# Attention's output products in three 16-bit terms, and a clamp written with two inputs

## The chip, the cores and the metric

The program runs on 1 core of one Trainium2 chip, in one launch. The metric is the device time of that core in microseconds, from the program's start to its end; lower is better. Three runs of the kernel before are shown, and one profiled execution, whose trace is read here.

## The reference, cut to what matters

Four layers follow one another on 2048 tokens of 128 numbers: an attention with 16 heads, a mixture of experts, a state space scan, and a second mixture. The change touches the attention alone, and in it the normalisation of queries and keys and the last product, `out @ w_out`.

```python
B, S, D, H, DH = 2, 1024, 128, 16, 64          # x as drawn: (2, 1024, 128)
q = (x @ w_q).reshape(b, s, h, -1).transpose(0, 2, 1, 3)
k, v = jnp.split(x @ w_kv, 2, axis=-1)
q = _l2norm(q) * jnp.exp(scale)                # t / max(norm(t), 1e-12), per head
k = _l2norm(k)
attn = jax.nn.softmax(jnp.einsum('bhid,bhjd->bhij', q, k), axis=-1)
out = jnp.einsum('bhij,bhjd->bhid', attn, v)
out = out.transpose(0, 2, 1, 3).reshape(b, s, h * out.shape[-1])
attention = out @ w_out + b_out

x = _layernorm(x + attention(x))
x = _layernorm(x + mixture_of_8_experts(x))    # top 2, silu gate, 512 wide
x = _layernorm(x + state_space_scan(x))
x = _layernorm(x + second_mixture(x))          # top 2 of 8, and a shared expert
```

## The kernel before, in words

**Tiling.** `attention` works on 16 halves `h`, each with two heads of one of the two sequences and 16 slots long. Two halves make a pair `i`, so there are 8 pairs, 0 to 7, of 32 slots. In a slot, the scores of 256 queries against 512 keys are made, exponentiated, and multiplied with the values. Slots 0 to 15 of a pair are its even half, slots 16 to 31 its odd half; while they run, the projections and normalisation of the next half are prepared. `heads` runs the function `slot(i, s)` of each engine over all of them, and then 32 more slots (`TAIL`) without scores for what is left over, the tail.

**What each engine does in slot s.** TensorE: 8 score matmuls (L510, L511) of slot s, 24 value matmuls (L536, L538, L540) of slot s-3 (`LAG`), and at set slots projections (L477 to L479), transposes of queries and keys (L492), transposes of finished outputs (L550) and the output products (L558). ScalarE: the exponential (L699), copies out of the accumulators (L668, L669, L681) and the copy `OT` of the turned outputs (L688). VectorE: the low part of the exponentials (L815), for every slot but 1 and 15 of a half; and at set slots the normalisation (L788, L797, L802), the sums of squares (L774), their clamp (L778), the division of finished outputs (L834, L838) and the addition of an output product to the residual stream (L847). GpSimd: the low parts for slots 1 and 15 (L1044), the power that gives inverse norms (L1051), low parts of values (L1059) and of normalised queries and keys (L1066). SyncE issues DMAs only.

**16-bit terms.** A product of 32-bit numbers is made in most places from three 16-bit products: high times high, high times low, low times high. The high part of a 32-bit tile that stays in place is its upper half read as bf16 (`high(...)[:, 1::2]`), the low part is the difference in f16. The output products (L558) are an exception: one matmul of 128x128 f32 for each of two blocks of 128 tokens, which the trace shows as two records each.

**Order.** Every engine runs its instructions in the order in which the code writes them, and waits on counting semaphores. The slots are tables of numbers: the output products of pair i, units u = 0 to 7, stand at `OUT_AT` = 41, 44, 47, 50, 57, 59, 61, 63, counted from the pair's first slot, so they run in the next pair at its slots 9, 12, 15, 18, 25, 27, 29 and 31; I name a product by its number here (P41 to P63). The turned outputs are read at `OUT_TURN_AT`. `SUM_AT` = 1, 4, 6, 8 places sum and clamp in each half, `NORM_AT` = 4, 6, 8, 10 the normalisation. Within a slot VectorE does the low part first, then the addition of a product, then normalisation and sum, then, every second slot, the division. TensorE may run ahead of VectorE: a value matmul of slot s-3 needs only that slot's low part.

**Waits around the change.** A product waits for its turned outputs (`s_out_turned_read`, ScalarE) and, since all products share the bank M0, for the addition of the one before (`s_out_added`, VectorE). In the tail two banks alternate. The clamp waits for its sum; the power on GpSimd waits for the clamp.

Of the kernel before, what the change touches and what calls it, by code (L numbers as in the profile page):

```python
# [4 lines left out]
F32 = mybir.dt.float32  # L5
# [25 lines left out]
def wait(eng, sem, count):  # L31

    if not isinstance(count, int) or count > 0:
        eng.wait_ge(sem, count)
# [29 lines left out]
TAIL = 32  # L64
RESIDUAL_AT = 14


# [47 lines left out]
def out_slot(u):  # L115

    return OUT_AT[u]


# [131 lines left out]
def attention(nc, io, t):  # L251
# [3 lines left out]
    def sb(name, shape, dt):  # L255
        return es.enter_context(nc.sbuf_tensor(name, shape, dt))
# [4 lines left out]
    with es:  # L261
# [3 lines left out]
        xT_lo = sb("xT_lo", [P, T], F16)  # L265
        wo = sb("wo", [P, H // 2 * D], F32)
        esc = sb("esc", [P, H], F32)
# [13 lines left out]
        Ob = sb("Ob", [P, NT, 2 * DH], F32)  # L281
        OT = sb("OT", [P, PJ, 2, P], F32)
        half = t["half"]
        bout = sb("bout", [P, D], F32)
# [37 lines left out]
        s_qk_high = sem("s_qk_high")  # L322
        s_k_copied = sem("s_k_copied")
        s_qk_low = sem("s_qk_low")
        s_turned = sem("s_turned")
# [102 lines left out]
        def _(eng):  # L428
            for c in range(WCH):
                eng.dma_start(w_f32[:, chunk(c)], io["wqkv"][:, chunk(c)]).then_inc(s_w_loaded[c], 16)  # L430
                if c == 0:
# [3 lines left out]
                    eng.dma_start(scl[:, :], io["scale"].partition_broadcast(P)).then_inc(s_loaded["scl"], 16)  # L435
            eng.dma_start(wo[:, :], io["wout"]).then_inc(s_loaded["wo"], 16)
            eng.dma_start(t["x"][:, :, :], io["x"].rearrange("(t p) d -> p t d", p=P)).then_inc(s_loaded["x"], 16)
# [19 lines left out]
        def _(eng):  # L457
# [95 lines left out]
            def out_product(i, u):  # L553

                wait(eng, s_out_turned_read, 8 * i + u + 1)
                for r in range(2):
                    pair = (2 * i + u // 4) % TB
                    mm = eng.matmul(out_bank(i, u)[:, P * r:P * r + P], OT[:, u, r, :],  # L558
                                    wo[:, D * pair:D * pair + D], start=True, stop=True)
                mm.then_inc(s_out_product, 1)  # L560
# [88 lines left out]
            for j in range(PJ):  # L649
                m1_free(0, j, 0, 0)  # L650
                transposes(0, j)
            eng.wait_ge(s_loaded["wo"], 16)
            eng.wait_ge(s_squares, PJ)
# [3 lines left out]
        def _(eng):  # L657
# [27 lines left out]
            def read_out_transposes(i, u):  # L685

                wait(eng, s_out_turned, 8 * i + u + 1)
                eng.activation(OT[:, u, :, :], out_turn_bank(i, u).rearrange("p (r c) -> p r c", r=2), ACT.Copy).then_inc(  # L688
                    s_out_turned_read, 1)
# [80 lines left out]
        def _(eng):  # L770
            def square_sums(h, hb, g):
                G, b = 4 * h + g, g % 2
                wait(eng, s_squares, 8 * h + 2 * g + 2)
                eng.tensor_reduce(ss[:, b, :, :], sq[:, b, :, :, :], AX, ALU.add).then_inc(s_square_sums, 1)  # L774

                wait(eng, s_square_sums, G + 1)
                wait(eng, s_inverse_norms, G - 1)
                eng.tensor_scalar(ss2[:, b, :, :], ss[:, b, :, :], 1e-24, None, ALU.max).then_inc(s_clamped, 1)  # L778

# [48 lines left out]
            def read_out(i, s):  # L828
# [10 lines left out]
                                  rden[:, u % 4, :].unsqueeze(2).to_broadcast([P, 2, DH]), ALU.mult).then_inc(  # L839
                                      s_outputs, 1)  # L840

            def add_out(i, u):
# [131 lines left out]
            def slot(i, s):  # L974
# [3 lines left out]
                if isinstance(i, int) and i == 0:  # L978

                    if s == RESIDUAL_AT:  # L980
                        start_residual()
                if (x := out_unit(s, out_slot)) and exists(i, x[0]):
                    if isinstance(i, int) and i < 2:
                        eng.wait_ge(s_residual, 1)
                    add_out(i - x[0], x[1])
# [1119 lines left out]
```

## Time and profile before

| | |
|---|---|
| median of 3 runs | 1048.07 us (1045.07 to 1051.78) |
| profiled execution | 1048.55 us, span 1046.8 us |
| TensorE busy | 914.1 us, 87% |
| ScalarE busy | 768.9 us, 73% |
| VectorE busy | 731.9 us, 70% |
| GpSimd busy | 499.3 us, 48% |
| attention | from 0 to about 636 us |

The span is the time from the first to the last instruction of the program; what is around it took 1.75 us in the profiled execution. Busy TensorE time is the union of matmuls whose ends are modelled, so that short waits between matmuls do not show in it; the starts of the matmuls in the timeline do. A short operation on VectorE starts some 0.08 us before the record of the one in front ends, so its step (start to start) is shorter than its record.

### The profile page before, as it was taken

To read this page: it belongs to the slowest core of one execution; us is meant where nothing else is said; L and a number is where in the kernel's file an instruction comes from. 1 tells how busy PE (TensorE), PEld (TensorE's weight loads), DVE (VectorE), ACT (ScalarE), POOL (GpSimd) and SP (SyncE) were. 2 spreads that over 40 slices of the span, in tenths; PEclk is the share of its full clock that TensorE was granted. 3 is DMA by queue.
4 is the path that set the end of the run, shared out by engine and by line. 5 is a ranking of instruction groups with operands and counts; after the bars stand their busy time and mean duration, and the time that the engine had idled before them with its cause. 6 is when DMAs were issued, how large, how long until landed. Compare 5 with 4: busy or idle time off the path is not lost. (4 is left out here: it accounts for less than half of the span.)

```text
span 1046.8 us, 34708 instructions
## 1 busy us (share of the span) xinstructions
PE 914.1 (87%) x13676; PEld 859.4 (82%) x13676; DVE 731.9 (70%) x1432; ACT 768.9 (73%) x1275; POOL 499.3 (48%) x384
## 2 busy tenths in 40 slices
PE   3789999999999999999999988979979479899930
PEld 2678998998999989888889988979968479899830
DVE  6699989888988988888998975325569849400202
ACT  5679998998988999988889865435563456687831
POOL 5475655555554654644778800413346350052423
PEclk9799999999999999999999998989989589899975
DMA  8400000000000000000001020713110030023111
GB/s 255 130 2 3 23 3 22 3 3 22 3 3 22 3 3 23 3 3 23 9 11 35 12 63 9 233 50 91 48 31 26 6 94 2 16 72 97 57 56 43
DMA packets 43563, 42.13 MB, mean 40 GB/s; under 512 B 5648, under 2 KB 37392, under 8 KB 43408
## 3 DMA queue, kind: packets, MB, share of 16 engines
q1 hardware_dynamic: 39312, 31.51, 10.1%
q0 software_dynamic: 4096, 8.40, 2.6%
q8 instruction: 116, 1.90, 0.7%
q14 instruction: 39, 0.32, 0.1%
HBM read 25.60 MB, written 14.29 MB: 38 GB/s over the span
## 5 line engine op out<-in xcount | busy, mean ns | idle before, releaser
L699 ACT ACTIVATE Pr<-SC,nesc,esc 128x1024 f32<-128x1024 f32 x256 | 310.2, 1212 | 33.3 <-PE SC L511 23.0
L815 DVE TENSOR_TENSOR Pl<-Pr 128x1024 f16<-128x1024 f32 x224 | 293.2, 1325 | 41.4 <-ACT Pr L699 39.7
L510 PE MATMUL SC<-QK 128*128 128x256 f16 x1024 | 239.2, 274 | 1.0 <-ACT QK L681 1.0
L511 PE MATMUL SC<-QK 128*128 128x256 f16 x1024 | 239.2, 274 | 0.0
L536 PE MATMUL OP<-V,Pr 128*128 128x65 f16 x2048 | 215.0, 193 | 6.1 <-DVE Ob L838 5.9
L538 PE MATMUL OP<-V,Pr 128*128 128x64 f16 x2048 | 215.8, 195 | 0.0
L540 PE MATMUL OP<-V,Pl 128*128 128x65 f16 x2048 | 214.6, 192 | 0.0
L536 PEld LDWEIGHTS OP<-V,Pr 128*128 128x128 bf16 x2048 | 191.3, 97 | 12.8 <-issue 8.7
L538 PEld LDWEIGHTS OP<-V,Pr 128*128 128x128 bf16 x2048 | 190.3, 97 | 2.6
L540 PEld LDWEIGHTS OP<-V,Pl 128*128 128x128 f16 x2048 | 191.0, 99 | 0.0
L1066 POOL TENSOR_TENSOR stk<-nrm,stk 128x512 f16<-128x512 f32 x64 | 75.1, 1173 | 141.4 <-DVE stk L797 141.4
L1469 PE MATMUL DB<-wd,hid 128*128 (+1 forms) x864 | 127.1, 292 | 11.8 <-issue 7.4
L681 ACT ACTIVATE QK<-M 128x768 f16<-128x768 f16 x124 | 101.1, 816 | 33.6 <-PE M L492 33.4
L1983 POOL DMA_INDIRECT yg<-ys,slots x64 | 74.1, 1158 | 108.3 <-PE AB L1442 64.4
L1469 PEld LDWEIGHTS DB<-wd,hid 128*128 128x128 f32 x864 | 109.4, 198 | 16.4 <-issue 14.0
L1051 POOL TENSOR_TENSOR rn<-ss,half 128x8 f32<-128x8 f32 x64 | 108.6, 1696 | 17.6 <-DVE ss L778 11.2
L1044 POOL TENSOR_TENSOR Pl<-Pr 128x1024 f16<-128x1024 f32 x32 | 64.3, 2011 | 97.9 <-ACT Pr L699 97.9
L510 PEld LDWEIGHTS SC<-QK 128*128 128x128 f16 x1024 | 100.9, 99 | 10.3 <-issue 1.2
L511 PEld LDWEIGHTS SC<-QK 128*128 128x128 f16 x1024 | 100.7, 98 | 9.5
L1967 POOL DMA_INDIRECT xs<-split,slots x48 | 49.7, 1036 | 77.4 <-PE AB L1442 48.4
L1059 POOL TENSOR_TENSOR V<-raw,V 128x256 f16<-128x256 f32 x64 | 84.8, 1324 | 0.1
L492 PE MATMUL M<-ident,stk 128*128 128x128 f16 x768 | 65.7, 223 | 15.5 <-DVE QK L806 6.0
(227 smaller groups left out, 2168.4 us busy)
## 6 DMA issues: line engine op xcount, KB each, us to landing
ys<-yb SPq DMA_DIRECT2D x92, 64.0 KB
w_or_rows<-xs SPq DMA_DIRECT2D x12, 384.0 KB, 3.8
wst<-in_up SPq DMA_DIRECT2D x8, 512.0 KB
xs<-zero SPq DMA_DIRECT2D x2, 1472.0 KB
scratch<-in_up SPq DMA_DIRECT2D x4, 576.0 KB
wd<-in_wd SPq DMA_DIRECT2D x4, 576.0 KB
wd<-in_wd SPq DMA_DIRECT2D x4, 512.0 KB
QK<-in_wqkv SPq DMA_DIRECT2D x4, 384.0 KB, 7.5
```

Of the source, the lines that this page charges most:

```text
L510: eng.matmul(out, QK[:, b, 1, key:key + P], rhs, start=True, stop=False)
L511: mm = eng.matmul(out, QK[:, b, 2, key:key + P], rhs, start=False, stop=True)
L536: eng.matmul(OP[u % 2][:, at:at + 65], hi, V[:, b, tile, 0:65], start=first, stop=False, skip_group_check=True)
L538: eng.matmul(OP[u % 2][:, at:at + 64], hi, V[:, b, tile, 65:129], start=False, stop=False, skip_group_check=True)
L540: mm = eng.matmul(OP[u % 2][:, at:at + 65], lo, V[:, b, tile, 0:65], start=False, stop=last, skip_group_check=True)
L681: eng.activation(QK[:, hb, :, 2 * P * j:2 * P * j + 2 * P], M1[:, :].bitcast(F16)[:, 0:6 * P].rearrange("p (k c) -> p k c", k=3), ACT.Copy ...
L699: eng.activation(Pr[:, n % PB, :, :], SC[s % 2][:, :, :], ACT.Exp, bias=nesc[:, hd:hd + 1], scale=esc[:, hd:hd + 1]).then_inc(s_exps, 1)
L815: eng.tensor_tensor(Pl[:, n % PB, :, :].rearrange("p a b -> p (a b)"), pr, high(pr)[:, 1::2], ALU.subtract).then_inc(s_low_probs, 1)
L1051: eng.tensor_tensor(rn[:, b, :, :], ss2[:, b, :, :], half[:, 0:1].unsqueeze(2).to_broadcast([P, 4, 2]), ALU.pow).then_inc(s_inverse_norms, 1)
L1059: eng.tensor_tensor(v[:, :, DH + 1:2 * DH + 1], raw[:, g, :, 2 * DH:QKV], v[:, :, 0:DH], ALU.subtract).then_inc(s_v_low, 1)
L1066: eng.tensor_tensor(both[:, :, :, DH:2 * DH], nrm[:, b, :, :, :], both[:, :, :, 0:DH], ALU.subtract).then_inc(s_qk_low, 1)
L1469: mm = eng.matmul(DB[:, 0:D], hid[:, u % HR, P * c:P * c + P], wd[l][c][:, at], start=c == 0, stop=c == NC - 1)
```

## The change

The output weights are loaded into the first half of the tile `OT`, which is free before the first turned outputs, and VectorE splits them in slots 16 and 18 of pair 0 into `wo_hi` and `wo_lo` (f16). Each output product is now six matmuls of 128x128 with 16-bit operands in place of two with 32-bit operands, over three lines. The low part of the turned outputs, `OTl`, is a new subtraction on VectorE over 128x256, `low_out`, at the product's slot less 2; its place in the slot is behind the low part of the exponentials and ahead of the addition. The product waits for it (`s_out_low`) and no longer for ScalarE's copy directly. `OTl` has two buffers, so a low part also waits for the product two before it. ScalarE's copy waits for the product that read the same part of `OT` one pair before. TensorE no longer waits for the weights' DMA ahead of the loop; VectorE does so in slot 16, and ScalarE's first copy waits for the split. The clamp `max(ss, 1e-24)` becomes `max(max(ss, 1e-24), ss)`, an operation that reads `ss` twice.

```diff
@@ -63,6 +63,7 @@
 SCATTER_AT = ((11, 12, 14, 18, 19, 25, 27, 28, 30), (2, 3, 9, 11, 12, 14, 18))
 TAIL = 32
 RESIDUAL_AT = 14
+SPLIT_WO_AT = (16, 18)
 
 
 
@@ -115,6 +116,11 @@
 def out_slot(u):
 
     return OUT_AT[u]
+
+
+def low_slot(u):
+
+    return OUT_AT[u] - 2
 
 
 def out_unit(s, place):
@@ -263,7 +269,8 @@
         w_lo = t["w_or_rows"][:, H * QKV:2 * H * QKV]
         xT_hi = sb("xT_hi", [P, T], F16)
         xT_lo = sb("xT_lo", [P, T], F16)
-        wo = sb("wo", [P, H // 2 * D], F32)
+        wo_hi = sb("wo_hi", [P, H // 2 * D], F16)
+        wo_lo = sb("wo_lo", [P, H // 2 * D], F16)
         esc = sb("esc", [P, H], F32)
         scl = sb("scl", [P, H], F32)
         nesc = sb("nesc", [P, H], F32)
@@ -280,6 +287,8 @@
         rden = sb("rden", [P, 4, 2], F32)
         Ob = sb("Ob", [P, NT, 2 * DH], F32)
         OT = sb("OT", [P, PJ, 2, P], F32)
+        OTl = sb("OTl", [P, 2, 2 * P], F16)
+        wo = OT[:, 0:H // 4, :, :].rearrange("p u r c -> p (u r c)")
         half = t["half"]
         bout = sb("bout", [P, D], F32)
         w_f32 = QK[:, 1, :, :].rearrange("p k t -> p (k t)").bitcast(F32)
@@ -321,6 +330,9 @@
         s_v_low = sem("s_v_low")
         s_qk_high = sem("s_qk_high")
         s_k_copied = sem("s_k_copied")
+        s_wo_high = sem("s_wo_high")
+        s_wo_low = sem("s_wo_low")
+        s_out_low = sem("s_out_low")
         s_qk_low = sem("s_qk_low")
         s_turned = sem("s_turned")
         s_outputs = sem("s_outputs")
@@ -433,7 +445,7 @@
                         cs = slice(S * m, S * m + S)
                         eng.dma_start(xT_f32[:, cs], io["xT"][:, cs]).then_inc(s_x_loaded[m], 16)
                     eng.dma_start(scl[:, :], io["scale"].partition_broadcast(P)).then_inc(s_loaded["scl"], 16)
-            eng.dma_start(wo[:, :], io["wout"]).then_inc(s_loaded["wo"], 16)
+            eng.dma_start(wo, io["wout"]).then_inc(s_loaded["wo"], 16)
             eng.dma_start(t["x"][:, :, :], io["x"].rearrange("(t p) d -> p t d", p=P)).then_inc(s_loaded["x"], 16)
             eng.dma_start(bout[:, :], io["b_out"].partition_broadcast(P)).then_inc(s_loaded["x"], 16)
             constants.sync(eng)
@@ -552,11 +564,15 @@
 
             def out_product(i, u):
 
-                wait(eng, s_out_turned_read, 8 * i + u + 1)
+                wait(eng, s_out_low, 8 * i + u + 1)
                 for r in range(2):
                     pair = (2 * i + u // 4) % TB
-                    mm = eng.matmul(out_bank(i, u)[:, P * r:P * r + P], OT[:, u, r, :],
-                                    wo[:, D * pair:D * pair + D], start=True, stop=True)
+                    out = out_bank(i, u)[:, P * r:P * r + P]
+                    hi, lo = high(OT[:, u, r, :])[:, 1::2], OTl[:, u % 2, P * r:P * r + P]
+                    wh, wl = wo_hi[:, D * pair:D * pair + D], wo_lo[:, D * pair:D * pair + D]
+                    eng.matmul(out, hi, wh, start=True, stop=False)
+                    eng.matmul(out, hi, wl, start=False, stop=False)
+                    mm = eng.matmul(out, lo, wh, start=False, stop=True)
                 mm.then_inc(s_out_product, 1)
 
             def early(i, s):
@@ -649,7 +665,6 @@
             for j in range(PJ):
                 m1_free(0, j, 0, 0)
                 transposes(0, j)
-            eng.wait_ge(s_loaded["wo"], 16)
             eng.wait_ge(s_squares, PJ)
             heads(eng, slot)
 
@@ -685,6 +700,9 @@
             def read_out_transposes(i, u):
 
                 wait(eng, s_out_turned, 8 * i + u + 1)
+                if (i, u) == (0, 0):
+                    eng.wait_ge(s_wo_low, 1)
+                wait(eng, s_out_product, 8 * (i - 1) + u + 1)
                 eng.activation(OT[:, u, :, :], out_turn_bank(i, u).rearrange("p (r c) -> p r c", r=2), ACT.Copy).then_inc(
                     s_out_turned_read, 1)
 
@@ -775,7 +793,8 @@
 
                 wait(eng, s_square_sums, G + 1)
                 wait(eng, s_inverse_norms, G - 1)
-                eng.tensor_scalar(ss2[:, b, :, :], ss[:, b, :, :], 1e-24, None, ALU.max).then_inc(s_clamped, 1)
+                eng.scalar_tensor_tensor(out=ss2[:, b, :, :], in0=ss[:, b, :, :], scalar=1e-24, in1=ss[:, b, :, :],
+                                         op0=ALU.max, op1=ALU.max).then_inc(s_clamped, 1)
 
             def normalize(h, hb, g):
                 G, b = 4 * h + g, g % 2
@@ -838,6 +857,22 @@
                 eng.tensor_tensor(Ob[:, rows:rows + 2, DH * k:DH * k + DH], o[:, :, 0:DH],
                                   rden[:, u % 4, :].unsqueeze(2).to_broadcast([P, 2, DH]), ALU.mult).then_inc(
                                       s_outputs, 1)
+
+            def split_out_weights(s):
+
+                if s == SPLIT_WO_AT[0]:
+                    eng.wait_ge(s_loaded["wo"], 16)
+                    eng.tensor_copy(wo_hi[:, :], wo).then_inc(s_wo_high, 1)
+                if s == SPLIT_WO_AT[1]:
+                    eng.wait_ge(s_wo_high, 1)
+                    eng.tensor_tensor(wo_lo[:, :], wo, wo_hi[:, :], ALU.subtract).then_inc(s_wo_low, 1)
+
+            def low_out(i, u):
+
+                wait(eng, s_out_turned_read, 8 * i + u + 1)
+                wait(eng, s_out_product, 8 * i + u - 1)
+                o = OT[:, u, :, :].rearrange("p r c -> p (r c)")
+                eng.tensor_tensor(OTl[:, u % 2, :], o, high(o)[:, 1::2], ALU.subtract).then_inc(s_out_low, 1)
 
             def add_out(i, u):
 
@@ -979,6 +1014,9 @@
 
                     if s == RESIDUAL_AT:
                         start_residual()
+                    split_out_weights(s)
+                if (x := out_unit(s, low_slot)) and exists(i, x[0]):
+                    low_out(i - x[0], x[1])
                 if (x := out_unit(s, out_slot)) and exists(i, x[0]):
                     if isinstance(i, int) and i < 2:
                         eng.wait_ge(s_residual, 1)
```

Line numbers in the rows of the change are its own: L834 there is L815 before, L853 and L857 are L834 and L838, L882 is L847, L875 is the new low part; on TensorE L573 to L575 are the product, L504 is L492, L522 and L523 are L510 and L511.

VectorE in slots 12 to 16 of a pair's even half, before (Pl is the low part of the exponentials, Ob the divided outputs, x the residual stream):

```order
L847 TENSOR_TENSOR x<-x,M 128x256
L834 RECIPROCAL rden<-OP 128x2
L838 TENSOR_TENSOR Ob<-OP,rden 128x2x64
L815 TENSOR_TENSOR Pl<-Pr 128x1024 x2
L834 RECIPROCAL rden<-OP 128x2
L838 TENSOR_TENSOR Ob<-OP,rden 128x2x64
L847 TENSOR_TENSOR x<-x,M 128x256
L815 TENSOR_TENSOR Pl<-Pr 128x1024
```

and now:

```order
L882 TENSOR_TENSOR x<-x,M 128x256
L853 RECIPROCAL rden<-OP 128x2
L857 TENSOR_TENSOR Ob<-OP,rden 128x2x64
L834 TENSOR_TENSOR Pl<-Pr 128x1024
L875 TENSOR_TENSOR OTl<-OT 128x256
L834 TENSOR_TENSOR Pl<-Pr 128x1024
L853 RECIPROCAL rden<-OP 128x2
L857 TENSOR_TENSOR Ob<-OP,rden 128x2x64
L882 TENSOR_TENSOR x<-x,M 128x256
L834 TENSOR_TENSOR Pl<-Pr 128x1024
L875 TENSOR_TENSOR OTl<-OT 128x256
```

A low part OTl stands between the low parts of slots 13 and 14, and one behind slot 16's; a third one, not shown, stands in slot 10 and a fourth in slot 7.

TensorE around P44, before, with the semaphores that each row waits for:

```order
L540 MATMUL OP<-V,Pl 128x65
L558 MATMUL M<-wo,OT 128x128 [waits s_out_turned_read_at,s_out_added_at,s_squares_at]
L558 MATMUL M<-wo,OT 128x128
L492 MATMUL M<-ident,stk 128x128 [waits s_qk_high_at,s_k_copied_at,s_out_turned_read_at,s_qk_low_at,s_turned_read_scalar_at,s_turned_read_vector_at]
L492 MATMUL M<-ident,stk 128x128 x5
L510 MATMUL SC<-QK 128x256 [waits s_exps_at]
```

and now:

```order
L552 MATMUL OP<-V,Pl 128x65
L573 MATMUL M<-wo_hi,OT 128x128 [waits s_out_low_at,s_out_added_at,s_squares_at]
L574 MATMUL M<-wo_lo,OT 128x128
L575 MATMUL M<-wo_hi,OTl 128x128
L573 MATMUL M<-wo_hi,OT 128x128
L574 MATMUL M<-wo_lo,OT 128x128
L575 MATMUL M<-wo_hi,OTl 128x128
L504 MATMUL M<-ident,stk 128x128 [waits s_qk_high_at,s_k_copied_at,s_out_turned_read_at,s_qk_low_at,s_turned_read_scalar_at,s_turned_read_vector_at]
L504 MATMUL M<-ident,stk 128x128 x5
L522 MATMUL SC<-QK 128x256 [waits s_exps_at]
```

The product waits for `s_out_low`, VectorE's, where it waited for `s_out_turned_read`, ScalarE's; two instructions have become six.

VectorE in the tail, before:

```order
L834 RECIPROCAL rden<-OP 128x2
L838 TENSOR_TENSOR Ob<-OP,rden 128x2x64
L847 TENSOR_TENSOR x<-x,M 128x256
L847 TENSOR_TENSOR x<-x,SC 128x256
L847 TENSOR_TENSOR x<-x,M 128x256
L847 TENSOR_TENSOR x<-x,SC 128x256
```

and now:

```order
L853 RECIPROCAL rden<-OP 128x2
L857 TENSOR_TENSOR Ob<-OP,rden 128x2x64
L875 TENSOR_TENSOR OTl<-OT 128x256
L882 TENSOR_TENSOR x<-x,M 128x256
L875 TENSOR_TENSOR OTl<-OT 128x256
L882 TENSOR_TENSOR x<-x,SC 128x256
L875 TENSOR_TENSOR OTl<-OT 128x256
L882 TENSOR_TENSOR x<-x,M 128x256
L875 TENSOR_TENSOR OTl<-OT 128x256
L882 TENSOR_TENSOR x<-x,SC 128x256
L875 TENSOR_TENSOR OTl<-OT 128x256 x2
```

The additions of the last eight products stood behind one another; now a low part stands between any two of them, and two between the fourth and the fifth. The low part of the sixth product is thus ahead of the fifth's addition, and so on to the last.

## Rows read from the trace of the kernel before

**Rows 1.** the page's first line.
```profile
span 1046.8 us, 34708 instructions
```

**Rows 2.** the view by windows, within pairs 2 and 3: busy us by engine.
```profile
core 0: us, PE busy (x) PEld busy (x) DVE busy (x) ACT busy (x) POOL busy (x), PEclk, DMA share, GB/s
240.00:310.00 70.00, 68.83 (x1219) 65.19 (x1217) 60.83 (x105) 63.75 (x93) 37.75 (x27) 1.00 0.04 10
```

**Rows 3.** the groups by line, 0 to 680 us: count, busy us, mean ns.
```profile
L778 DVE TENSOR_SCALAR ss<-ss 128x8 f32<-128x8 f32 x64 | 29.0, 453 | 2.2
```

**Rows 4.** the timeline of TensorE (start us, duration us, operation): even half, pair 3.
```profile
276.51 0.69 PE L558 MATMUL M<-wo,OT 128*128 128x128 f32 x4
277.04 0.50 PE L492 MATMUL M<-ident,stk 128*128 128x128 f16 x6
277.38 0.27 PE L510 MATMUL SC<-QK 128*128 128x256 f16 x1
...
289.24 0.69 PE L558 MATMUL M<-wo,OT 128*128 128x128 f32 x4
```

**Rows 5.** the timeline of VectorE, pair 3, even half, same columns.
```profile
265.14 1.23 DVE L815 TENSOR_TENSOR Pl<-Pr 128x1024 f16<-128x1024 f32 x1 [1.13 <-ACT Pr L699]
...
271.27 1.15 DVE L788 TENSOR_TENSOR nrm<-raw,rn 128x512 f32<-128x512 f32 x1
...
279.16 0.44 DVE L778 TENSOR_SCALAR ss<-ss 128x8 f32<-128x8 f32 x1
...
282.52 0.68 DVE L788 TENSOR_TENSOR nrm<-raw,rn 128x512 f32<-128x512 f32 x1
...
288.23 2.35 DVE L815 TENSOR_TENSOR Pl<-Pr 128x1024 f16<-128x1024 f32 x2
...
292.08 1.33 DVE L815 TENSOR_TENSOR Pl<-Pr 128x1024 f16<-128x1024 f32 x1 [0.77 <-ACT Pr L699]
```

**Rows 6.** the timeline of GpSimd, the same stretch.
```profile
270.37 1.50 POOL L1059 TENSOR_TENSOR V<-raw,V 128x256 f16<-128x256 f32 x1
...
278.41 1.17 POOL L1066 TENSOR_TENSOR stk<-nrm,stk 128x512 f16<-128x512 f32 x1 [1.09 <-DVE stk L797]
...
289.98 2.35 POOL L1044 TENSOR_TENSOR Pl<-Pr 128x1024 f16<-128x1024 f32 x1 [3.49 <-ACT Pr L699]
```

**Rows 7.** the timeline of TensorE, odd half, pair 3; idle time in brackets.
```profile
312.00 0.61 PE L558 MATMUL M<-wo,OT 128*128 128x128 f32 x4
312.89 0.27 PE L492 MATMUL M<-ident,stk 128*128 128x128 f16 x2 [0.28 <-issue]
...
317.89 0.68 PE L558 MATMUL M<-wo,OT 128*128 128x128 f32 x4 [0.52 <-issue]
...
322.73 0.68 PE L558 MATMUL M<-wo,OT 128*128 128x128 f32 x4 [0.27 <-issue]
```

**Rows 8.** the timeline of VectorE in that half: additions of products.
```profile
317.38 0.41 DVE L847 TENSOR_TENSOR x<-x,M 128x256 f32<-128x256 f32 x1
317.71 1.22 DVE L815 TENSOR_TENSOR Pl<-Pr 128x1024 f16<-128x1024 f32 x1
...
322.23 0.41 DVE L847 TENSOR_TENSOR x<-x,M 128x256 f32<-128x256 f32 x1
```

**Rows 9.** the timeline of TensorE, last eight products.
```profile
628.99 1.19 PE L558 MATMUL M<-wo,OT 128*128 128x128 f32 x4 [1.01 <-ACT OT L688]
...
632.49 0.68 PE L558 MATMUL M<-wo,OT 128*128 128x128 f32 x4
```

**Rows 10.** the timeline of VectorE, first and last of their additions.
```profile
630.22 0.42 DVE L847 TENSOR_TENSOR x<-x,M 128x256 f32<-128x256 f32 x1 [5.61 <-PE M L558]
...
634.98 0.42 DVE L847 TENSOR_TENSOR x<-x,SC 128x256 f32<-128x256 f32 x1
```

**Rows 11.** the timeline of VectorE, pair 0, slots 17 and 18.
```profile
77.22 0.17 DVE L778 TENSOR_SCALAR ss<-ss 128x8 f32<-128x8 f32 x1
78.58 1.22 DVE L815 TENSOR_TENSOR Pl<-Pr 128x1024 f16<-128x1024 f32 x1 [1.19 <-ACT Pr L699]
```

## The prediction

> **What bounds the kernel now.** The attention takes 636 of the 1046.8 us [rows 1], and nothing outside it changes. I read the windows first: in steady pairs TensorE is busy for 68.83 of 70 us, ScalarE 63.75, VectorE 60.83 [rows 2]. TensorE looks like the bound, with VectorE at 87% as one that shouldn't matter. So I looked for where VectorE's idle time lies. In the even half it starts at 265.14, after a wait for an exponential, and its next idle time is the 0.77 ahead of 292.08, from 291.31 on [rows 5]. For 26 us it is full, and TensorE, up to three slots ahead, lives on that distance. In the odd half the distance is already used up: P59 and P61 start at 317.89 and 322.73 behind idle times of 0.52 and 0.27 [rows 7], just after the additions of 317.38 and 322.23 end (317.79, 322.64) [rows 8]; they wait for the bank that VectorE frees. VectorE's work is thus cheap in slots 15 to 20 and costs time in the rest. That is where the change puts its low parts.
>
> **Part 1, the product on TensorE.** From P41 to the next transposes it is 277.04 - 276.51 = 0.53 us; six f16 matmuls with 128 columns take 277.38 - 277.04 = 0.34 [rows 4], which is the new product's form. Saved 0.19 us, 64 times 12.2 us, where TensorE is what ends last.
>
> **Part 2, the low part on VectorE.** No row shows it; the nearest are the addition with the same 128x256, 0.41 us [rows 8], and the low part of exponentials with 128x1024 and the same kinds of operands, 1.23 us [rows 5]. A quarter of the latter, 0.31, would leave out the fixed part, so it is the lower bound; I take 0.41 for the record and 0.33 for the step, as records overlap by some 0.08. In all 21 us of VectorE's time.
>
> **Even half.** A product needs a low part two slots back, while value products need one three slots back. For P47 it is that of slot 13. Its exponentials' low part is the first of the two at 288.23, whose step ends at 288.23 + 2.35 - 1.22 = 289.36 [rows 5]. The low parts put into slots 7 and 10 push this by 0.66 to 290.02, the one of slot 13 takes 0.41, and with 0.07 for the semaphore P47 starts at 290.50 where it started at 289.24 [rows 4]: 1.26 late (P44's smaller lateness is in it). P47 and P50 give back 0.38. A margin of 1.3 us would be needed and there is none. Left: +0.88 us an even half, of which there are seven with products: +6.2. VectorE's idle 0.77 ahead of 292.08 [rows 5] takes in its own extra work, so nothing is carried on by it.
>
> **Odd half.** P57 becomes 0.4 late, but the transposes behind it wait until 312.89 anyway [rows 7]: nothing. P59 waits for the addition of 317.38, which now has two low parts more ahead of it, P61 for that of 322.23 with three: +0.99. P61 and P63 give back 0.38. Left +0.61, six times: +3.7. In pair 7 nothing is prepared in the odd half and VectorE has room: four products faster, -0.8.
>
> **Tail.** From the first of the last eight products, 628.99, to the fifth, 632.49, it is 3.50 us, two banks hiding the additions [rows 9]. Now low part u stands behind addition u-1 on VectorE, so that each of four steps is product to addition, 0.56 us (0.34 and the rest of a matmul's record, 0.50 - 0.28 [rows 4]) up to 0.9 (the first row is slower, 1.19 against 0.68 for four records [rows 9]), addition 0.33, low part 0.41, semaphores 0.07: 1.37 to 1.71, four times 5.5 to 6.8. That is +2.0 to +3.3; I take +2.5. The last three overlap as before: 634.98 stays 2.5 after the fifth [rows 9, 10]. VectorE's additions begin at 630.22 only [rows 10]; all behind waits for the last.
>
> **The weights' split.** A cast and a subtraction of 128x1024, by the low part's 1.23 [rows 5] at most 2.4 us together, in pair 0. Ahead of slot 18 VectorE idles 1.19 us [rows 11], and three slots follow without normalisation: 0. Uncovered it costs up to 1.2. That TensorE no longer waits for their DMA I cost at nothing: no idle time in the trace is put down to it.
>
> **The clamp.** It takes 0.44 us at 279.16, ending at 279.60, for 8 elements, and GpSimd's L1066 runs from 278.41 to 279.58 [rows 5, 6]. The mean over 64 is 453 ns [rows 3]. So it stands still until GpSimd's instruction ends; where GpSimd is between two instructions it takes 0.17 [rows 11], 0.27 less. Does a second input free it? L788 reads two tiles in SBUF: it takes 0.68 us at 282.52, but 1.15 at 271.27 while L1059 runs until 271.87 [rows 5, 6]. Operations with two inputs wait as well, so I take 0; the other bound is -0.27, three times in each full stretch (slots 4, 6, 8); slot 1's clamp lies where VectorE has room. The Trainium skill, SBUF — State Buffer, Who interferes with whom, says the same of any VectorE instruction with two SBUF inputs against a GpSimd instruction that reads SBUF, and calls the lock exclusive. By that rule the clamp gains nothing; the trace agrees for L788, with 1.15 against 0.68 us.
>
> **Sum.** 6.2 + 3.7 - 0.8 + 2.5 = +11.6 us. The profiled execution took 1048.55 us, its span and 1.75 around it, 0.5 over the median of 1048.07. Predicted: 1060 us. About 1% either way is what a measurement can tell from no change: 1037.6 to 1058.6 counts as the same.
>
> **Rivals.**
> - *The clamp gets free.* 0.81 us less on VectorE in each full stretch. P47 is then 0.45 late less 0.38: +0.07. In the odd half P61 is 0.18 late less 0.38: -0.20. Seven and six times: -0.7, less 0.8, and +2.5 for the tail: 1050 us, not slower by 1%. For it: an operation with two inputs doesn't run in the mode in which a one-input one may take both ports. Against it: L788. Chance 0.2.
> - *VectorE's load doesn't matter*, because the waits that GpSimd gives it shrink when its work moves. Then 12.2 are saved, less 2.5: 1039 us; with the clamp free as well, and the waits of the odd half gone (0.79 each [rows 7], six times), 1034. For it: 13% idle VectorE time [rows 2]; against it: no idle time between 265.14 and 291.31. Chance 0.14.
> - *GpSimd gets in ahead.* L1044 of slot 15 asks at 289.98 and ran only when VectorE let go [rows 6]; the new low part of slot 13 starts at 290.02. If exponentials are not late by P44's stall, GpSimd is first and holds VectorE for some 1.8 us of the 2.35. P47 is then late by 1.8 more, seven times 12: 1072 us. I hold it for second, since that exponential is itself 0.2 late. Chance 0.14.
> - *Forecast*: 0.52, with its own range of 1054 to 1067, from the low part's 0.31, the tail's bounds and P44's share.
>
> **Numbers.** The range of 1043 to 1072 leaves out most of the second rival and the upper half of the third, some 0.2. Slower: most of the forecast and the third, 0.58. Same: the first, most of the second and the forecast's lower edge, 0.34. Faster: 0.08.
>
> **What would show it.** After: the product's step 0.34; L875 at about 0.41; L796 still near 0.44 beside GpSimd; P47 behind an idle time of about 1 us that the low part ends, P61 about 0.8 later against its half's start; a pair from P41 to P41 longer by about 1.5 us; from the first to the last of the eight final additions about 7.3 us where it was 634.98 - 630.22 = 4.76 [rows 10]. A clamp of 0.17 us makes the first rival right; idle time of VectorE ahead of each L875 the third; a shorter pair the second.

## The result

The change runs in 1064.99 us (median; 1064.07 to 1066.70 in four runs), the kernel before in 1047.68 (1045.07 to 1051.78). The ratio is 1.0163, 95% interval 1.0128 to 1.0199: slower by 1.6%. The forecast was 1060, its range 1043 to 1072. The profiled execution took 1065.49 us, and its span of 1063.8 is 17.0 over the 1046.8 of before [rows 1].

**The profile after.** The page's first lines:

```profile
span 1063.8 us, 35148 instructions
## 1 busy us (share of the span) xinstructions
PE 910.0 (86%) x13804; PEld 849.7 (80%) x13804; DVE 754.8 (71%) x1498; ACT 769.2 (72%) x1275; POOL 494.9 (47%) x384
```

VectorE's busy time grew from 731.9 to 754.8 us. The new lines and the clamp, from the groups by line of the attention stage (count, busy us, mean ns, idle time before them):

```profile
L875 DVE TENSOR_TENSOR OTl<-OT 128x256 f16<-128x256 f32 x64 | 33.5, 525 | 0.0
L796 DVE SCALAR_TENSOR_TENSOR ss<-ss 128x8 f32<-128x8 f32 x64 | 28.0, 437 | 2.2
```

The clamp's mean went from 453 to 437 ns [rows 3], so it still waits for GpSimd. The low part's record is some 0.42 us in 49 of 64 places; in the other 15 it is 0.87 to 0.89, each time beside a GpSimd subtraction; so its mean is 525 ns.

Next the list of waits, 0 to 656 us: who waited for what, us in total, times, longest. Three entries for TensorE in the kernel before, then the first three in the change:

```profile
PE OP L536 <- DVE Ob L838: 5.9, 9, 2.5
PE M L558 <- issue: 4.6, 10, 1.1
PE M L477 <- DVE x L847: 1.7, 3, 0.8
```

```profile
PE M L573 <- DVE x L882: 12.9, 13, 1.9
PE OP L548 <- DVE Ob L857: 10.4, 15, 2.5
PE M L573 <- DVE OTl L875: 8.8, 16, 1.3
```

The longest wait of the change is new, and all three are for VectorE operations: the addition that frees the products' bank (12.9 us), the division (10.4, was 5.9), and the new low part (8.8).

**P47.** The timelines of VectorE and TensorE at the step that the prediction singles out (start us, duration us, operation, idle time before it):

```profile
293.87 1.22 DVE L834 TENSOR_TENSOR Pl<-Pr 128x1024 f16<-128x1024 f32 x1
295.00 0.42 DVE L875 TENSOR_TENSOR OTl<-OT 128x256 f16<-128x256 f32 x1
295.34 1.22 DVE L834 TENSOR_TENSOR Pl<-Pr 128x1024 f16<-128x1024 f32 x1
```

```profile
295.57 0.22 PE L573 MATMUL M<-wo_hi,OT 128*128 128x128 f16 x1 [0.57 <-DVE OTl L875]
```

The low part ends at 295.42 and P47 starts 0.15 later. The half began at 259.37, so P47 comes 36.20 after it, where it came 289.24 - 254.40 = 34.84 after it before: 1.36 late.

**P61**, in the odd half:

```profile
327.26 1.80 DVE L834 TENSOR_TENSOR Pl<-Pr 128x1024 f16<-128x1024 f32 x1
328.98 0.87 DVE L875 TENSOR_TENSOR OTl<-OT 128x256 f16<-128x256 f32 x1
329.77 0.41 DVE L882 TENSOR_TENSOR x<-x,M 128x256 f32<-128x256 f32 x1
```

```profile
327.93 1.64 POOL L1097 TENSOR_TENSOR V<-raw,V 128x256 f16<-128x256 f32 x1
```

GpSimd's subtraction runs from 327.93 to 329.57. The low part asks at 328.98 and ends at 329.85, 0.28 after GpSimd does: 0.87 us for work of 0.42.

**Where the 17.0 us lie**, by the first score matmul of each half in the two timelines (us by which the change is later; a pair's even half is its first; the last value is 14.95 in full):

```
pair            0     1     2     3     4     5     6     7
even half     0.0   0.8   3.1   5.0   7.3   9.5  12.6  13.6
odd half      0.9   2.0   3.8   6.1   8.4   9.6  13.9  14.9
```

The last addition is 653.54 - 634.98 = 18.56 late [rows 10], and the part behind the attention gives back 1.6.

Two of these numbers are not the change's. The 0.9 at the first odd half (69.53 us in the change) is there before VectorE begins the weights' split at 76.15, and the version below with nothing changed but the clamp has 0.97 at that place. In both the granted clock was at its lower level until 40.6 and 40.9 us, in the kernel before until 38.1, and the lateness arises in the slots up to there. From the last addition to the end the fourteen profiles of this document range from 407.9 to 412.4 us, so 1.6 is within what one execution differs from another.

A third is the clock's in part. Pair 5's odd half loses 3.0 us, more than any other. TensorE stands there for 1.89 us until 486.65, for an addition, and is busy for 1.91 of the 3.80 us up to 487.80; from then to 491.20 the granted clock is 0.50, the 1.2 GHz level, and TensorE is busy throughout. Slot 14 starts 11.1 us late, slot 15, behind it, 12.4: 1.3 of the 3.0 us. The kernel before has a granted clock of 1.00 in that half.

**The tail.** VectorE and TensorE in its first steps, and then the window over it (us, busy us by engine, granted clock as PEclk):

```profile
644.18 0.42 DVE L882 TENSOR_TENSOR x<-x,M 128x256 f32<-128x256 f32 x1 [4.98 <-PE M L575]
644.52 0.42 DVE L875 TENSOR_TENSOR OTl<-OT 128x256 f16<-128x256 f32 x1
645.92 0.42 DVE L882 TENSOR_TENSOR x<-x,SC 128x256 f32<-128x256 f32 x1 [0.98 <-PE SC L575]
```

```profile
643.35 0.27 PE L573 MATMUL M<-wo_hi,OT 128*128 128x128 f16 x1 [0.84 <-issue]
...
645.09 0.27 PE L573 MATMUL SC<-wo_hi,OT 128*128 128x128 f16 x1 [0.94 <-DVE OTl L875]
...
646.83 0.27 PE L573 MATMUL M<-wo_hi,OT 128*128 128x128 f16 x1 [0.94 <-DVE OTl L875]
```

```profile
core 0: us, PE busy (x) PEld busy (x) DVE busy (x) ACT busy (x) POOL busy (x), PEclk, DMA share, GB/s
640.00:655.00 15.00, 7.17 (x52) 5.06 (x52) 6.02 (x19) 3.86 (x7) 0.00 (x0) 0.55 0.00 0
645.00:650.00 5.00, 2.39 (x18) 1.68 (x18) 2.11 (x6) 1.06 (x2) 0.00 (x0) 0.50 0.00 0
```

A step (product, addition, low part, product) takes 1.74 us: 0.83 from the product's start to the addition's, at the lower clock, 0.34 to the low part's start, 0.42 for the low part, and 0.15 to the next product. From first to last addition it is 9.36 us, where it was 4.76 [rows 10].

### The profile page after: what moved, and what is told of

Its sections match the earlier page's. It is cut to its first block and busy times, and to the rows that moved or that the text cites. A ratio compares the mean times of both kernels' runs of the same rounds, so it can differ in the third digit from the quotient of the medians.

```text
span 1063.8 us, 35148 instructions
## 1 busy us (share of the span) xinstructions
PE 910.0 (86%) x13804; PEld 849.7 (80%) x13804; DVE 754.8 (71%) x1498; ACT 769.2 (72%) x1275; POOL 494.9 (47%) x384
## 5 line engine op out<-in xcount | busy, mean ns | idle before, releaser
L834 DVE TENSOR_TENSOR Pl<-Pr 128x1024 f16<-128x1024 f32 x224 | 293.0, 1319 | 40.0 <-ACT Pr L717 37.6
L522 PE MATMUL SC<-QK 128*128 128x256 f16 x1024 | 240.0, 275 | 1.0 <-ACT QK L696 1.0
L523 PE MATMUL SC<-QK 128*128 128x256 f16 x1024 | 239.9, 275 | 0.0
L548 PE MATMUL OP<-V,Pr 128*128 128x65 f16 x2048 | 215.4, 193 | 10.6 <-DVE Ob L857 10.4
L1507 PE MATMUL DB<-wd,hid 128*128 (+1 forms) x864 | 125.5, 290 | 11.6 <-DVE x L1847 5.5
L1082 POOL TENSOR_TENSOR Pl<-Pr 128x1024 f16<-128x1024 f32 x32 | 67.4, 2107 | 99.2 <-ACT Pr L717 99.1
L522 PEld LDWEIGHTS SC<-QK 128*128 128x128 f16 x1024 | 101.2, 99 | 10.6 <-issue 1.2
L523 PEld LDWEIGHTS SC<-QK 128*128 128x128 f16 x1024 | 100.9, 98 | 9.3
L1097 POOL TENSOR_TENSOR V<-raw,V 128x256 f16<-128x256 f32 x64 | 78.4, 1224 | 0.1
L504 PE MATMUL M<-ident,stk 128*128 128x128 f16 x768 | 66.2, 224 | 13.9 <-DVE QK L825 6.0
```

The source lines that it names most:

```text
L522: eng.matmul(out, QK[:, b, 1, key:key + P], rhs, start=True, stop=False)
L523: mm = eng.matmul(out, QK[:, b, 2, key:key + P], rhs, start=False, stop=True)
L548: eng.matmul(OP[u % 2][:, at:at + 65], hi, V[:, b, tile, 0:65], start=first, stop=False, skip_group_check=True)
L834: eng.tensor_tensor(Pl[:, n % PB, :, :].rearrange("p a b -> p (a b)"), pr, high(pr)[:, 1::2], ALU.subtract).then_inc(s_low_probs, 1)
L1097: eng.tensor_tensor(v[:, :, DH + 1:2 * DH + 1], raw[:, g, :, 2 * DH:QKV], v[:, :, 0:DH], ALU.subtract).then_inc(s_v_low, 1)
L1507: mm = eng.matmul(DB[:, 0:D], hid[:, u % HR, P * c:P * c + P], wd[l][c][:, at], start=c == 0, stop=c == NC - 1)
```

## The experiments

The theory: VectorE has no slack from slot 5 or so of a half to its end, and the low parts stand there; the shorter products and the clamp decide nothing. The rivals are named in each expectation. A ratio is that to the kernel before, with its 95% interval. The diffs are cut to the lines that matter; buffers, semaphores and the order of the tail are left out.

### Which part of the change costs

**The clamp alone** (kernel before, with the clamp of the change):

```diff
-eng.tensor_scalar(ss2[:, b, :, :], ss[:, b, :, :], 1e-24, None, ALU.max)
+eng.scalar_tensor_tensor(out=ss2[:, b, :, :], in0=ss[:, b, :, :], scalar=1e-24, in1=ss[:, b, :, :],
+                         op0=ALU.max, op1=ALU.max)
```

> The kernel before with the clamp alone written with two inputs. Theory: the clamp waits for GpSimd's instruction in either form, so its record stays near 0.43 to 0.44 us beside L1066, and the time stays within 1 us of before. Rival (the two-input form is dearer, and part of the slowdown is its): 64 clamps of 0.5 us or more and +3 us or more. Rival (it gets free): 0.17 us, and some -3 us.

Measured 1047.33 us, ratio 1.0001 (0.9984 to 1.0019). Nothing, as forecast; the clamp's mean is 0.45 us.

**The products alone** (the change, with the same line turned back):

> The changed kernel with the clamp back in its one-input form. Theory: all 17 us come from the output products, so this is within 1 us of the changed kernel, +17 against before. Rival: if the clamp has a share, this is faster than the changed kernel by that share, 3 us or more.

Measured 1064.61 us, 1.0180 (1.0154 to 1.0205): all of the loss.

**The load alone** (kernel before with its f32 products, and the 64 low parts that nobody reads):

```diff
+if (x := out_unit(s, low_slot)) and exists(i, x[0]):
+    low_out(i - x[0], x[1])
```

> The kernel before with the 64 low parts put on VectorE in the same slots, but used by nobody: the products stay 32-bit and do not wait for them. It tells VectorE's load from the new wait. Theory (both count): in the even half TensorE no longer waits for a low part two slots back, so P47 is late by 0.1 to 0.3 only; in the odd half P59 and P61 still wait for additions that two and three low parts push back, +1.0 to +1.4 each odd half; six of them give +6 to +9, tail +0.3: about 1056. If the load were all: 17 us and the 12 that the faster products give back, 1070 or more. If the wait were all: 1048.

Measured 1060.14 us, 1.0135 (1.0107 to 1.0164), more than expected. Its last half starts 13.4 us late, the change's 14.9; counted from the start of pair 1, behind the uneven beginning, they are 14.3 and 14.2 late. So VectorE's time alone, with no product waiting for a low part, brings a loss in the attention as large as the change's. That the wait costs nothing isn't shown by it: the change has the shorter products as well, which may pay for the wait. The tails differ: 6.75 us from the first product to the last addition here, 10.19 in the change, where the products do wait.

**The products without the load** (VectorE forms no low part; the third term reads zeros):

```diff
-wait(eng, s_out_low, 8 * i + u + 1)
+wait(eng, s_out_turned_read, 8 * i + u + 1)
...
-if (x := out_unit(s, low_slot)) and exists(i, x[0]):
-    low_out(i - x[0], x[1])
```

> The change without the low parts: VectorE forms none, and the third term of every product reads a buffer of zeros; the six 16-bit matrix products and the splitting of the weights stay (leaves out the low part of the attention outputs). Theory A (the 16-bit form itself is a gain while TensorE sets the pace: 0.19 us less for each of 64 products, 12 us at most, less about 1 us for the splitting of the weights): 1036 to 1041 us. Rival D (TensorE's time in a half is given back as a wait for VectorE's chain): 1044 to 1047 us.

Measured 1047.74 us, 1.0000 (0.9986 to 1.0014). Here theory A's number fell: the 12.2 us of shorter products come to nothing. The first odd half starts 1.2 us late, before the weights' split, which begins at 76.39; its clock rose at 41.0. The products then make pairs 1 to 3 0.4 us shorter each, of 1.5 saved, and the last half starts 1.3 early: 2.4 us gained from pair 1's start on. The timeline of TensorE in pair 3's odd half shows at P59 where the rest goes:

```profile
318.15 0.22 PE L572 MATMUL M<-wo_hi,OT 128*128 128x128 f16 x1 [0.52 <-issue]
```

It has the same 0.52 us of idle time as before [rows 7], and again starts 0.10 us after the end of VectorE's addition (318.05). What TensorE saves, it mostly waits for VectorE in the next place. In the last half a new stall of 2.1 us takes what was left (shown below, at the five-buffer version, which has it too).

### Does it matter where the low parts stand?

**Earlier, four buffers**, at slots 31 to 34 and 47 to 50 of the pair's count:

```diff
-    return OUT_AT[u] - 2
+    return OUT_LOW_AT[u]      # (31, 32, 33, 34, 47, 48, 49, 50)
```

> The changed kernel with the low parts moved to slots where VectorE has idle time (slots 31 of the own pair, and 0, 1, 2, 15, 16, 17 and 18 of the next), with four buffers for them, and in the tail ahead of the chain of additions. Work and form are those of the changed kernel. Theory: the loss was placement, so no product waits for its low part; the additions are where they were before, TensorE keeps 4 times 0.19 us in each half that it bounds, the tail is no longer a chain of product, addition, low part: 1040 to 1046. Rival (the load counts wherever it stands, or six 16-bit matmuls are not cheaper in place): 1055 or more.

Measured 1069.35 us, 1.0225 (1.0203 to 1.0247): worse than the change. That version's timelines of VectorE, GpSimd and TensorE, pair 3, around the start of the odd half:

```profile
297.19 1.71 DVE L877 TENSOR_TENSOR OTl<-OT 128x256 f16<-128x256 f32 x1
298.82 0.41 DVE L884 TENSOR_TENSOR x<-x,M 128x256 f32<-128x256 f32 x1
```

```profile
296.08 2.54 POOL L1087 TENSOR_TENSOR Pl<-Pr 128x1024 f16<-128x1024 f32 x1 [3.30 <-ACT Pr L719]
```

```profile
299.37 0.24 PE L491 MATMUL M<-w_or_rows,xT_hi 128*128 128x192 f16 x1 [1.78 <-DVE x L884]
```

VectorE is free at slots 15 and 0 because GpSimd forms the exponentials' low part for slot 15 then. A low part put there waits until 298.62, when GpSimd ends, and takes 1.71 us. Such low parts of 1.7 us or more are 15 of the 64. Behind it stands the addition, and behind that a projection that needs the bank: TensorE stands for 1.78 us. Over the attention such waits of projections are 19.8 us, where they were 1.7.

**Three slots ahead instead of two:**

```diff
-    return OUT_AT[u] - 2
+    return OUT_AT[u] - 3
```

> The change with the low parts formed three slots ahead of their products instead of two (same 64 low parts on VectorE, same products). Theory A (VectorE's chain in the second part of each half is what is longer: 0.42 to 0.88 us for each low part, whatever the lead): the time stays, 1061 to 1066 us. Rival B (what costs is that a product waits for a low part made just before it, with 0.15 us from its end to the product's start): 1052 to 1058 us.

Measured 1069.83 us, 1.0216 (1.0197 to 1.0235). Both numbers missed, and the cause is the same: P50's low part falls on slot 15 and takes 1.71 us there.

```profile
298.53 1.71 DVE L875 TENSOR_TENSOR OTl<-OT 128x256 f16<-128x256 f32 x1
300.16 0.41 DVE L882 TENSOR_TENSOR x<-x,M 128x256 f32<-128x256 f32 x1
```

In pairs 1 to 3 the odd half loses 1.9 us in its first slot, and 2.6 in all, where the change's loses 1.1 to 1.2.

**In VectorE's real gaps**, two at a time at slots 1 and 3 of each half, where VectorE idles and GpSimd rests or is only about to start. One gap is the 1.13 us ahead of 265.14 [rows 5], the other, from the timeline of before:

```profile
259.86 0.69 DVE L774 TENSOR_REDUCE ss<-sq 128x8 f32<-128x512 f32 x1 [1.42 <-ACT sq L669]
```

```diff
+OUT_LOW_AT = (33, 33, 35, 35, 49, 49, 51, 51)
```

> The change with the low parts moved, two at a time, into stretches in which VectorE stands idle in the kernel before (before the first sum of squares and after the low part of the fourth head, in each half: slots 1 and 3), with four buffers, and in no slot in which GpSimd's two-input operation runs just before an addition. Theory A (the load costs only where it stands ahead of an addition or behind GpSimd; in an idle stretch it costs nothing): 1036 to 1044 us, the kernel before less what the shorter products give. Rival C (VectorE has no slack anywhere, each 0.42 us comes back at the half's end): 1056 to 1064 us.

Measured 1053.31 us, 1.0057 (1.0039 to 1.0075). That is 11.7 less than the change with the same work. VectorE in pair 3:

```profile
258.71 0.75 DVE L872 TENSOR_TENSOR OTl<-OT 128x256 f16<-128x256 f32 x2
260.11 0.69 DVE L789 TENSOR_REDUCE ss<-sq 128x8 f32<-128x512 f32 x1 [0.64 <-ACT sq L681]
```

Two low parts for 0.75 us, and still 0.64 idle. From pair 1's start to pair 5's it gains 0.6 us on the kernel before and the version with zeros 1.4, so its low parts cost 0.8 there, for four pairs. It loses 1.6 us in pair 5's even half and 2.3 in pair 6's odd half, where VectorE forms other things in those slots. In these two halves a low part takes 2.11 us (at 405.89) and 2.33 us (at 524.64) beside GpSimd's operations, and in the second the granted clock is 0.5 from 530.1 to 533.5, where one slot alone becomes 1.5 us later. The last half loses 1.6, but so does that of the version with zeros: this isn't the low parts'. The expected 1036 to 1044 assumed the gain of the products, which the zeros disprove.

**The same, but two slots ahead in those two halves**, and five buffers, so that the tail's first five low parts are formed before its products:

```diff
+    near = (i == 4 and u < 4) or (i == 5 and u > 3)
+    return OUT_AT[u] - 2 if near else OUT_LOW_AT[u]
```

> The low parts in VectorE's idle stretches (slots 1 and 3 of each half), except for the two halves in which VectorE forms other things there (even half of pair 5, odd half of pair 6), where they stay two slots ahead of their products; five buffers, and in the tail five of them formed before the products begin. Theory A (placed where VectorE idles, low parts cost nothing; the +1.7, +2.3 and some 2 us that the version with all in idle stretches lost in those two halves and in the tail go): 1045 to 1048 us. Rival C (they come back elsewhere): 1051 to 1054 us.

Measured 1050.87 us, 1.0030 (1.0013 to 1.0047), between the two expectations. The last half starts 0.5 us late instead of 3.2, as meant. The rest is not in the tail, as I had it: from first product to last addition there are 637.45 - 631.17 = 6.28 us, before 634.98 - 628.99 = 5.99 [rows 9, 10]. With the low parts formed ahead, the chain of the change's tail (10.19 us) is thus gone. What is left lies in the last half's slot 3. VectorE and GpSimd in this version, then VectorE in the kernel before:

```profile
594.96 5.49 DVE L837 TENSOR_TENSOR Pl<-Pr 128x1024 f16<-128x1024 f32 x1
600.37 0.16 DVE L856 RECIPROCAL rden<-OP 128x2 f32<-128x2 f32 x1
```

```profile
595.00 1.90 POOL L1090 TENSOR_TENSOR Pl<-Pr 128x1024 f16<-128x1024 f32 x1
596.85 0.67 POOL L1105 TENSOR_TENSOR V<-raw,V 128x256 f16<-128x256 f32 x1
597.47 1.89 POOL L1090 TENSOR_TENSOR Pl<-Pr 128x1024 f16<-128x1024 f32 x1
```

```profile
597.70 2.93 DVE L815 TENSOR_TENSOR Pl<-Pr 128x1024 f16<-128x1024 f32 x1
```

VectorE's low part begins with GpSimd's first operation and ends 1.1 us after its third, which ends at 599.36: 5.49 us for work of 1.22. Before, it got in between GpSimd's operations. TensorE then idles 1.93 us up to 601.00 for the division. The version with zeros (5.50 us) and the one before this (5.47) have the same stall, the change and the kernel before don't. Slot 4 of the last half is 2.1 us later by it, slot 15 still 1.6.

**On GpSimd**, same slots:

> The change with the 64 low parts of the outputs formed by GpSimd instead of VectorE, in the same slots. Theory A (what costs is VectorE's time, and GpSimd is busy 47% only; each low part of 128x256 on GpSimd takes about 0.65 us as its 128x256 subtraction at L1059 does at its shortest, and VectorE's two-input operations wait for it now and then): 1050 to 1057 us. Rival E (a low part on GpSimd stands behind its own 1.6 to 2.9 us operations, the product waits for it, and it locks VectorE out for longer than the 0.42 us saved): over 1065 us.

Measured 1061.58 us, 1.0144 (1.0123 to 1.0165): neither. GpSimd in pair 3, and TensorE at P41:

```profile
277.12 1.64 POOL L1087 TENSOR_TENSOR rn<-ss,half 128x8 f32<-128x8 f32 x1
278.72 1.47 POOL L1081 TENSOR_TENSOR OTl<-OT 128x256 f16<-128x256 f32 x1
```

```profile
280.33 0.22 PE L573 MATMUL M<-wo_hi,OT 128*128 128x128 f16 x1 [0.76 <-POOL OTl L1081]
```

The low part stands behind a 1.64 us power and takes 1.47 (mean 1.07 over 64, shortest 0.61). TensorE waits 23.6 us for GpSimd's low parts in all: VectorE's load is gone, and latency takes its place.

### What VectorE's time is worth

**A clamp with one input**, in the kernel before: the maximum over pairs of the sum and a stored 1e-24.

```diff
-eng.tensor_scalar(ss2[:, b, :, :], ss[:, b, :, :], 1e-24, None, ALU.max)
+eng.tensor_reduce(ss2[:, b, :, :], ss[:, b, :, :, :], AX, ALU.max)
```

> The kernel before with the clamp written as a maximum over pairs (the sum and 1e-24 beside it), an operation with one input. Theory: the clamp waits for GpSimd or not, but nothing on TensorE waits for it: 1045 to 1048 us. Rival (the clamp frees itself from GpSimd, 0.25 us less 64 times on VectorE's chain in the stretches that set the pace): 1035 to 1042 us.

Measured 1040.93 us, 0.9942 (0.9923 to 0.9961). The rival had it. The group of that line:

```profile
L778 DVE TENSOR_REDUCE ss<-ss 128x8 f32<-128x16 f32 x64 | 10.9, 170 | 2.2
```

Every one of the 64 takes 0.17 us: it never waits for GpSimd. That frees 18.1 us of VectorE (29.0 less 10.9), and a third of it shows in the time, 6.1 us by the ratio. The gain lies in the odd half, 0.83 us each in pairs 1 to 3, between slots 11 and 12; even halves gain nothing. The Trainium skill, SBUF — State Buffer, Who interferes with whom, says that on this chip a reduction has no mode that takes the shared ports and never contends; the trace agrees, with 0.17 against 0.45 us for the same eight elements. The number of inputs isn't what frees it: the clamp of before has one input as well, and waits.

**The same edit in the change:**

> The change with the clamp written as a maximum over pairs, an operation with one input, 0.17 us each where the clamp of the change takes 0.44. Theory A (VectorE's chain sets the pace in the second part of both halves in the change, of one half in the kernel before, where the same edit gave 6 us): 1051 to 1058 us, a gain of 7 to 14. Rival F (VectorE's chain is not what sets the end, the products' waits are): 1062 to 1066 us.

Measured 1054.22 us, 1.0064 (1.0043 to 1.0086): 10.4 us less than the products with the clamp of before (1064.61, 1.0180), by the ratios 12, against 6.1 without the low parts. TensorE's wait for the division fell from 10.4 to 3.8 us:

```profile
PE OP L548 <- DVE Ob L856: 3.8, 3, 2.5
```

**Both together**, low parts in the gaps and the reduced clamp:

> The same with the clamp as a maximum over pairs (one input). Theory A (the low parts cost nothing, and the freed clamp gives its 6 us here too, with perhaps 1 or 2 us of the shorter products behind it): 1037 to 1042 us, faster than both kernels. Rival C: over 1045 us.

Measured 1038.37 us, 0.9922 (0.9906 to 0.9937), the fastest here: faster than both kernels, with three 16-bit terms. Against the reduced clamp alone (0.9942) the intervals overlap.

## Why the prediction held, step by step

- **What bounds the kernel**: right, and more so than I put it. "VectorE's work is cheap in slots 15 to 20 and costs time in the rest" holds by the load alone (+13.4) and by the gaps (-11.7). But "cheap in slots 15 to 20" was too wide: slots 15 and 0 are empty since GpSimd is at work, and cost most (1.71 us for 0.42). I read the idle time of one engine without asking what GpSimd did in it.
- **Product on TensorE**: it takes 0.33 (281.48 to 281.81), 0.34 foreseen, or some 0.19 less than before. That it counts only where TensorE is what ends last was right, but I let it count in every half: with zeros for the low parts, all 64 together give 0.0 us, with an interval of some 1.5 either way.
- **Low part**: 0.41 foreseen, 0.42 measured where GpSimd rests, 0.87 where it doesn't. I gave the wait for GpSimd a rival of its own (1.8 us, GpSimd getting in ahead at slot 15), but left its small form, 0.45 us in 15 of 64 places, out of the sum. The rival's own case did not occur in the change: at P47 VectorE was first, and GpSimd's slot-15 operation at 295.44 took 2.87 us. In three other versions its mechanism did, in the last half, for 2.1 us.
- **Even half**: forecast +0.88, seven times 6.2. P47 was 1.36 late against 1.26 foreseen; the seven halves sum to 7.0. They are less alike than this says: 0.7 to 1.4 in six of them, and 0.1 in pair 5.
- **Odd half**: the term that was mis-sized. Forecast +0.61, six times 3.7; measured 7.2 in sum, 1.1 to 1.2 in pairs 1 to 4, 3.0 in pair 5, and -0.3 in pair 6. P57 is 0.4 late and P59 0.6, about as foreseen; P61 is 1.4 late against its half's start, where two steps of 0.33 and a third were to make 0.99. The third low part is what differs: from its start to the addition's it is 329.77 - 328.98 = 0.79 us, beside GpSimd, and not 0.33. (The exponentials' low part in front of it, 1.80, took 1.79 before.) Pair 5, where VectorE also forms other low parts and the clock fell, was not in the sum.
- **Pair 7's odd half**: -0.8 foreseen, 643.35 - 628.99 - 14.95 = -0.6 measured.
- **Tail**: +2.5 foreseen within 2.0 to 3.3, 18.56 - 14.36 = 4.2 measured. Four steps make 6.95 us for 3.50 [rows 9], 3.45 more. A step was 1.74 where I allowed 1.71 at most. Its first part, 0.83, lies within my 0.56 to 0.9, near the upper end: the granted clock was 0.50, the 1.2 GHz level, in all of 645 to 650 us, and TensorE was busy for 2.39 of those 5. My 0.07 for the semaphore, for which no row stood, was 0.15. The last three products took 3.24 for 2.49, which I had called unchanged: 0.75 more.
- **Weights' split**: 0 foreseen, with 1.2 as the bound. The cast alone takes 2.4 us and the subtraction 1.2, more than the 2.4 I had for both; but pair 0's odd half, in which they stand, takes 0.1 less than before, so 0 was right.
- **Clamp**: 0 foreseen; 1.0001 measured.
- **Sum**: 0.9 up to the first odd half, -0.1 in it, 7.0, 7.2, -0.6 and 4.2 make 18.6, less 1.6 behind the attention: 17.0 in place of 11.6. The mechanism held, but a third of the loss was missing from the sum, and the time lies in the range since the range was wide. Too small were the odd half (by 3.5) and the tail (by 1.7), since I had left out what GpSimd and the clock do while VectorE and TensorE wait. The 0.9 and the 1.6, which I hadn't forecast and which differ from one execution to another, nearly cancel: that is luck.
- **The signs**: idle time ahead of P47 was 0.57 us, not about 1; P61 was 1.4 us later, not 0.8; pair 3 was longer by 2.3 us, not 1.5; the eight final additions took 9.36 us, not 7.3. L875 and L796 were as forecast.

## What to carry to other kernels

An engine at 87% can be the bound for most of each period. Ask where its idle time lies and why; a gap in which another engine's operation holds this one up is not free, and work put there can cost four times its length. A saving on the engine that looks busiest is worth nothing if it then waits for the other. A tiny operation that is repeated often and stands behind another engine's (8 elements, 0.45 us) can be the cheapest thing to mend. And look at the granted clock behind a long wait: here TensorE waited for 1.9 us, and in the lower clock behind it a slot lost 1.3 more.

## What the runs showed of the hardware that I had not expected

- A reduction over a pair, one SBUF input, took 0.17 us 64 times out of 64, beside the same GpSimd work that held the two other forms of the clamp to 0.44 and 0.45 us on average.
- VectorE stood for three GpSimd operations in a row, 5.49 us in one record. In the kernel before, where GpSimd's first of them began at 594.19, 0.29 ahead of VectorE's, the two took turns; here it began 0.04 behind, and 0.02 and 0.05 behind in the two others with the stall. A shift of a third of a microsecond went with 2.1 us of delay. Who goes first when both wait, these runs don't settle.
- The same 128x256 subtraction took 0.42, 0.87 or 1.71 us, by what GpSimd had begun before it, and 5.2 us once each in two versions, beside three GpSimd operations in a row.
- From the end of a VectorE operation to the start of the matmul that waits for it: 0.15 us behind a low part (295.42 to 295.57), 0.10 behind an addition (317.79 to 317.89 before). I had reckoned 0.07.
- With GpSimd's own two-input operation on 128x256, 1.47 us were seen beside 0.61 at its shortest, where VectorE's low parts of the exponentials ran until 279.72, a second into it. That it waits for VectorE as VectorE waits for it fits this, but was not tested.
- The granted clock is at its lower level from some 20 us until 38.1 to 41.2 us in the fourteen profiles, and again for 3.4 us from 74 to 76 us on in eight of them. The version with the load alone, one of the other six, starts pair 1 0.95 us early, the one with the clamp alone 0.84 late, though neither has changed products. Lateness is better counted from pair 1 on.
